# A shared feed-forward stage by pairs of token tiles: inner rows made transposed, logits in four column groups

## What is computed

```python
logits = xf @ w_gate.T                                  # 4096 x 8
scores = softmax(logits)
...                                                     # top groups, top 2 experts
shared = silu(xf @ sw1.T) * (xf @ sw3.T) @ sw2.T        # 512 -> 512 -> 512
out = shared.at[flat_idx].add(routed_out)
x = x + out
```

## Time and profile before

| | |
|---|---|
| median of 3 runs | 2368.78 us (2368.17 to 2370.43) |
| profiled execution, its own time | 2368.74 us |
| its span | 2367.0 us |
| TensorE matmul busy | 2099.7 us, 89% of the span |
| VectorE, ScalarE, GpSimd busy | 1451.2, 1072.9, 671.0 us |
| mean granted TensorE clock | 0.957 of full speed |
| the shared stage, first turn of x to last row out | 1922.7 to about 2253 us |

### The profile page before, as it was taken

The page is one execution under the profiler, slowest core; times in us unless marked ns, Lnnn a source line. Parts: engine busy times, 40 slices in busy tenths (PEclk is TensorE's granted clock), DMA queues, the critical chain, the costliest instruction groups (busy, mean ns, idle before and its releaser), DMA issues. The chain is left out here.

```text
span 2367.0 us, 47476 instructions
## 1 busy us (share of the span) xinstructions
PE 2099.7 (89%) x14941; PEld 1593.7 (67%) x14976; DVE 1451.2 (61%) x4087; ACT 1072.9 (45%) x2781; POOL 671.0 (28%) x1179
## 2 busy tenths in 40 slices
PE   5998999899998379898995899999999979999986
PEld 4777777677776344444443788888888768888844
DVE  5777777777777377777773565655655533333354
ACT  4566566556656533333342445444454422222224
POOL 1233233223322355555552221212212111111100
PEclk8999999999999589999997899999999989999999
DMA  5011121111100611212114012112121083222100
GB/s 173 31 47 39 47 66 38 38 68 45 38 23 23 231 50 54 66 53 66 58 53 152 29 37 73 64 44 72 36 72 54 28 280 118 74 79 76 66 10 0
DMA packets 91344, 158.11 MB, mean 67 GB/s; under 512 B 11248, under 2 KB 21488, under 8 KB 90752
## 3 DMA queue, kind: packets, MB, share of 16 engines
q1 hardware_dynamic: 91264, 157.10, 19.5%
HBM read 123.50 MB, written 33.57 MB: 66 GB/s over the span
## 5 line engine op out<-in xcount | busy, mean ns | idle before, releaser
L480 ACT ACTIVATE a_probs<-a_probs,a_negm 128x256 f32<-128x256 f32 x512 | 254.3, 504 | 179.1 <-DVE a_negm L581 179.1
L400 POOL TENSOR_SCALAR a_probs<-a_probs,a_rinv 128x256 f32<-128x256 f32 x256 | 130.3, 524 | 467.2 <-DVE a_rinv L597 467.0
L581 DVE CUSTOM_DVE_ANT_0 a_probs<-a_s,a_mbias 128x256 f32<-128x256 f32 x512 | 188.6, 417 | 12.7 <-PE a_s L801 12.7
L818 PE MATMUL a_pt<-a_ident,a_probs 128*128 128x128 f32 x1024 | 160.8, 281 | 19.3 <-DVE a_pT L590 7.8
L1125 ACT ACTIVATE b_raw<-b_g,b_xs 128x512 f32<-128x512 f32 x128 | 88.1, 688 | 181.9 <-PE b_g L1296 181.9
L1296 PE MATMUL b_u<-b_wu,b_raw 128*128 128x512 bf16 x495 | 130.7, 380 | 40.1 <-DVE b_raw L1208 39.2
L480 ACT ACTIVATE c_probs<-c_probs,c_negm 128x256 f32<-128x256 f32 x256 | 127.4, 502 | 83.2 <-DVE c_negm L581 83.2
L400 POOL TENSOR_SCALAR c_probs<-c_probs,c_rinv 128x256 f32<-128x256 f32 x128 | 64.9, 522 | 326.6 <-DVE c_rinv L597 326.4
L818 PEld LDWEIGHTS a_pt<-a_ident,a_probs 128*128 128x128 f32 x1024 | 124.1, 144 | 45.6 <-issue 22.9
L767 PE MATMUL a_x<-a_wo,a_oT 128*128 128x512 f32 x384 | 114.4, 447 | 23.8 <-DVE a_xnT L627 23.8
L1208 DVE SCALAR_TENSOR_TENSOR b_raw<-b_u,b_xs,b_raw 128x512 f32<-128x512 f32 x128 | 93.0, 745 | 62.2 <-ACT b_raw L1125 54.7
(11 more groups left out here) (297 smaller groups left out, 4981.1 us busy)
## 6 DMA issues: line engine op xcount, KB each, us to landing
m_ew<-in_L_ffn_w_dram SPq DMA_DIRECT2D x24, 512.0 KB, 8.9
a_cbuf<-in_ctx_dram SPq DMA_DIRECT2D x16, 512.0 KB, 5.3
a_xbuf<-in_x_dram SPq DMA_DIRECT2D x16, 512.0 KB, 4.2
a_resb<-in_x_dram SPq DMA_DIRECT2D x16, 512.0 KB, 3.6
x<-a_resb SPq DMA_DIRECT2D x16, 512.0 KB, 2.8
b_xbuf<-x SPq DMA_DIRECT2D x32, 256.0 KB, 2.7
b_raw<-x SPq DMA_DIRECT2D x32, 256.0 KB, 2.8
x<-b_raw SPq DMA_DIRECT2D x32, 256.0 KB, 2.0
```

Source lines behind the costliest of these rows:

```text
L400: last = nc.gpsimd.tensor_scalar(pr, pr, rinv[:, s, QT + t:QT + t + 1], 0.0, ALU.mult, ALU.add)
L480: nc.scalar.activation(pr, pr, ACT.Exp, bias=negm[:, s, h % 2, t:t + 1], scale=-1.0, accum_out=ssum[:, s, QT * (h % 2) + t:QT * (h % 2) + ...
L581: nc.vector.tensor_tensor_reduce(out=probs[:, s, h % 2, t], in0=s_bank[h][:, t * SEQ:(t + 1) * SEQ], in1=mbias[:, el.par], scale=-sm_scale ...
L818: last = nc.tensor.transpose(pt_bank[:, kt * SEQ + t * P:kt * SEQ + (t + 1) * P], probs[:, s, m, t, kt * P:(kt + 1) * P], ident[:])
```

## The change

The stage now works on 16 groups of two tiles (256 tokens).

- `gate` and `up` are made transposed: the weights are stationary (128 inner features at a time) and the 256 token columns of a pair move. Each is cut into two halves of 256 features (`features`), 24 matmuls of 256 columns a half. What `hidden` makes is thus already what `down` needs as stationary operand; `turn_h` and the bank `th` are gone, and `hi_h` and `lo_h` read `hid` from memory.
- `xnT` holds both tiles of a pair side by side, and `gate` of a pair's first half waits for `tx_lo` of both tiles.
- The logits are made transposed: `gateT` is padded to 32 columns and stationary, and the four chunks of 128 features go to the four groups of 32 columns of the array, into 128 partitions of the bank `lT`. ScalarE copies it (`logits_out`), and `fold_logits` adds up the four parts with a matmul by `fold`, which GpSimd now makes in this stage.
- Each tile of a pair has its own bank for `down`, `z0` and `z1`. x is loaded six tiles ahead, not four.

The diff, cut to its core, with the code's left margin taken off:

```diff
-gateT = tsb("gateT", [P, KC, EXPERTS])
+gateT = tsb("gateT", [P, KC, 32])
...
-xnT = tsb("xnT", [P, 2, 2, DIM], F32R)
-xnT_full = tsb("xnT_full", [P, 2, DIM])
+GROUP = 2 * P
+xnT = tsb("xnT", [P, 2, 2, KC, GROUP], F32R)
+xnT_full = tsb("xnT_full", [P, KC, GROUP])
+logitsT = tsb("logitsT", [P, GROUP])
...
-hidT = tsb("hidT", [P, 2, 2, DIM], F32R)
-tx_bank, th_bank, g_bank, u_bank, z_bank = [tbank(n) for n in ("tx", "th", "g", "u", "z")]
-w_bank = [tx_bank, th_bank, g_bank, u_bank]
+hidT = tsb("hidT", [P, 2, KC, GROUP], F32R)
+tx_bank, lT_bank, g_bank, u_bank = [tbank(n) for n in ("tx", "lT", "g", "u")]
+z_bank = [tbank("z0"), tbank("z1")]
+w_bank = [tx_bank, z_bank[1], g_bank, u_bank]
...
         def iteration(el):
-            if el.has(4):
-                load_x(el.plus(4))
+            if el.has(6):
+                load_x(el.plus(6))
...
-        def hi_h(el):
-            act.wait_ge(th_done, el.n + 1)
-            nc.scalar.activation(hidT[:, el.par, HI], th_bank[:], ACT.Copy).then_inc(th_hi, 1)
...
+        def hi_x(el, t):
+            n, cut = 2 * el.n + t, slice(t * P, (t + 1) * P)
+            act.wait_ge(tx_done, n + 1)
+            wait_for(act, lT_done, el.n)
+            src = tx_bank[:].rearrange("p (k n) -> p k n", k=KC)
+            nc.scalar.activation(xnT_full[:, :, cut], src, ACT.Copy).then_inc(tx_full, 1)
+            nc.scalar.activation(xnT[:, el.par, HI, :, cut], src, ACT.Copy).then_inc(tx_hi, 1)
...
+        def hi_h(el, half):
+            act.wait_ge(h_done, el.n * 2 + half + 1)
+            nc.scalar.activation(hidT[:, HI, 2 * half:2 * half + 2].rearrange("p j n -> p (j n)"),
+                                 hid[:, half], ACT.Copy).then_inc(h_hi, 1)
+
+        def logits_out(el):
+            act.wait_ge(lT_done, el.n + 1)
+            wait_for(act, lg_done, el.n)
+            nc.scalar.activation(logitsT[:], lT_bank[:, 0:GROUP], ACT.Copy).then_inc(lT_out, 1)
...
         def iteration(el):
-            if el.has(1):
-                silu(el.plus(1))
-            hi_h(el)
+            if not el.has(1):
+                return
+            silu(el.plus(1), 0)
+            logits_out(el.plus(1))
+            hi_h(el.plus(1), 0)
             if el.has(2):
-                hi_x(el.plus(2))
-
-        run_elements(act, tiles, iteration, ahead=4)
+                hi_x(el.plus(2), 0)
+            silu(el.plus(1), 1)
+            hi_h(el.plus(1), 1)
+            if el.has(2):
+                hi_x(el.plus(2), 1)
+
+        run_elements(act, groups, iteration)
...
+        def lo_x(el, t):
+            n, cut = 2 * el.n + t, slice(t * P, (t + 1) * P)
+            dve.wait_ge(tx_hi, n + 1)
+            nc.vector.tensor_tensor(xnT[:, el.par, LO, :, cut], tx_bank[:].rearrange("p (k n) -> p k n", k=KC),
+                                    xnT[:, el.par, HI, :, cut].bitcast(F32), ALU.subtract).then_inc(tx_lo, 1)
+
+        def hidden(el, half):
+            n = el.n * 2 + half
+            dve.wait_ge(silu_done, n + 1)
+            dve.wait_ge(u_done, n + 1)
+            wait_for(dve, h_hi, n - 1)
+            nc.vector.tensor_tensor(hid[:, half], u_bank[:], act_gate[:, half], ALU.mult).then_inc(h_done, 1)
+
+        def lo_h(el, half):
+            dve.wait_ge(h_hi, el.n * 2 + half + 1)
+            hi, lo = (hidT[:, part, 2 * half:2 * half + 2].rearrange("p j n -> p (j n)") for part in (HI, LO))
+            nc.vector.tensor_tensor(lo, hid[:, half], hi.bitcast(F32), ALU.subtract).then_inc(h_lo, 1)
+
+        def rows_out(el, t):
+            dve.wait_ge(r_loaded[t], el.n * 16 + 16)
+            dve.wait_ge(z_done, el.n * 2 + t + 1)
+            nc.vector.tensor_tensor(resb[:, t], z_bank[t][:], resb[:, t], ALU.add).then_inc(out_done, 1)
...
         def iteration(el):
-            lo_h(el)
-            if el.has(1):
-                hidden(el.plus(1))
-            if el.has(2):
-                lo_x(el.plus(2))
-            if el.has(3):
-                row_stats(el.plus(3))
-            rows_out(el)
+            rows_out(el, 0)
             if isinstance(el.n, int) and el.n == 0:
                 keep_first()
-
-        run_elements(dve, tiles, iteration, ahead=4)
+            rows_out(el, 1)
+            if not el.has(1):
+                return
+            hidden(el.plus(1), 0)
+            lo_h(el.plus(1), 0)
+            if el.has(2):
+                lo_x(el.plus(2), 0)
+            if el.has(3):
+                row_stats(Element(el.plus(3).n, 0, tiles))
+            hidden(el.plus(1), 1)
+            lo_h(el.plus(1), 1)
+            if el.has(2):
+                lo_x(el.plus(2), 1)
+            if el.has(3):
+                row_stats(Element(el.plus(3).n, 1, tiles))
+
+        run_elements(dve, groups, iteration, ahead=4)
...
+        def features(el, half, bank, w, done, read):
+            wait_for(pe, read, el.n * 2 + half)
+            for m in range(2):
+                j = 2 * half + m
+                for k in range(KC):
+                    for a, b in TERMS:
+                        last = nc.tensor.matmul(bank[:, m * GROUP:(m + 1) * GROUP],
+                                                w[:, b, k, j * P:(j + 1) * P], xnT[:, el.par, a, k],
+                                                start=(k == 0 and (a, b) == TERMS[0]),
+                                                stop=(k == KC - 1 and (a, b) == TERMS[-1]))
             last.then_inc(done, 1)
 
-        def turn_x(el):
-            pe.wait_ge(xn_ready, el.n + 1)
-            wait_for(pe, tx_lo, el.n)
-            turn(tx_bank, xn[:, el.par], tx_done)
-
-        def turn_h(el):
-            pe.wait_ge(h_done, el.n + 1)
-            wait_for(pe, th_lo, el.n)
-            turn(th_bank, hid[:, el.par], th_done)
-
-        def product(bank, srcT, w, done):
+        def gate(el, half):
+            if half == 0:
+                pe.wait_ge(tx_lo, 2 * el.n + 2)
+            features(el, half, g_bank, sw[0], g_done, silu_done)
+
+        def up(el, half):
+            features(el, half, u_bank, sw[1], u_done, h_done)
+
+        def logits(el):
+            pe.wait_ge(tx_full, 2 * el.n + 2)
+            wait_for(pe, lT_out, el.n)
+            for k in range(KC):
+                last = nc.tensor.matmul(lT_bank[32 * k:32 * k + 32, 0:GROUP], gateT[:, k], xnT_full[:, k],
+                                        start=True, stop=True, skip_group_check=True)
+            last.then_inc(lT_done, 1)
+
+        def fold_logits(el):
+            pe.wait_ge(lT_out, el.n + 1)
+            pe.wait_ge(fold_ready, 3)
+            for t in range(2):
+                n = 2 * el.n + t
+                last = nc.tensor.matmul(lg_bank[:, bass.ds(n * EXPERTS, EXPERTS)],
+                                        logitsT[:, t * P:(t + 1) * P], fold[:], start=True, stop=True)
+            last.then_inc(lg_done, 1)
+
+        def down(el, t):
+            pe.wait_ge(h_lo, el.n * 2 + 2)
+            wait_for(pe, out_done, el.n * 2 + t - 1)
             for k in range(KC):
                 for a, b in TERMS:
-                    last = nc.tensor.matmul(bank[:], srcT[:, a, k * P:(k + 1) * P], w[:, b, k],
+                    last = nc.tensor.matmul(z_bank[t][:], hidT[:, a, k, t * P:(t + 1) * P], sw[2][:, b, k],
...
+            last.then_inc(z_done, 1)
+
+        for t in range(2):
+            turn_x(first_group[0], t)
+        gate(first_group[0], 0)
+        logits(first_group[0])
+        up(first_group[0], 0)
+        fold_logits(first_group[0])
+        turn_x(first_group[1], 0)
+        gate(first_group[0], 1)
+        up(first_group[0], 1)
+        turn_x(first_group[1], 1)
 
         def iteration(el):
             if el.has(1):
+                gate(el.plus(1), 0)
                 logits(el.plus(1))
-                gate(el.plus(1))
-            turn_h(el)
+            down(el, 0)
             if el.has(1):
-                up(el.plus(1))
+                fold_logits(el.plus(1))
+            down(el, 1)
+            if el.has(1):
+                up(el.plus(1), 0)
             if el.has(2):
-                turn_x(el.plus(2))
-            down(el)
-
-        run_elements(pe, tiles, iteration, ahead=4)
+                turn_x(el.plus(2), 0)
+            if el.has(1):
```

More of the change, by code:

```diff
@@ L1379, in routed_ffn_phase @@
         first_ready = sem("first_ready")
+        fold = sb("fold", [P, EXPERTS])
+        fold_ready = sem("fold_ready")
         with ExitStack() as shared:
@@ L1420, in routed_ffn_phase @@
                          "r_loaded1 stored0 stored1 bn_done stats_ready ln_step xn_ready tx_done tx_hi tx_full "
-                         "tx_lo lg_done g_done u_done silu_done h_done th_done th_hi th_lo z_done out_done").split()]
+                         "tx_lo lT_done lT_out lg_done g_done u_done silu_done h_done h_hi h_lo z_done out_done").split()]
                 x_loaded, r_loaded, stored = (x_loaded0, x_loaded1), (r_loaded0, r_loaded1), (stored0, stored1)
                 w_loaded = [sem(f"sw_loaded{n}") for n in range(3)]
```

(30 more changed lines are left out.)

103 lines of the change are left out of this document (44 added, 59 removed).

## The result

The changed kernel takes 2438.74 us (median of 5 runs, 2436.81 to 2440.99) against 2370.14 of the kernel before on the same chip: ratio 1.0293, 95% interval 1.0278 to 1.0308, slower by 69 us. The forecast was slower by 48. Its mechanism is there, but the time lies 7 us above its range (2397 to 2432): the change costs some 20 us more than forecast, most of it at one place.

A forecast was written before the change was run, and what follows sets the result against it. TensorE's own stream was taken to bound the stage, 20.1 us a pair. Work -18, stall +45, clock falls +19 and edges +2 gave +48 us on 2368.74: 2417 us, range 2397 to 2432.

The forecast's parts named there:

- TensorE's work: Changed loop, matmul stream of a pair without waits: 19.0 us against 20.1, a gain of 18 us for 16 pairs.
- The stall: `gate` opening an iteration waits for the split of the x just turned: 3.0 us a pair, 15 times, 45 us.
- the chain named: From the second tile's turn: `hidden`, `hi_h`, second copy of x, `lo_x`, then `gate` 3.36 us after the turn starts.
- a stall of 2.1: Least wait before `gate`, if `hi_h` were not ahead: the chain from the turn alone, 0.64 + 1.81 us.
- The price of a fall: After a stall TensorE's clock may drop to half level; 3.4 us of that costs 1.6 us.
- The number: Clock falls expected behind the stalls before `gate`: 12 in 15, 19 us in all, bounds 0 and 47.
- Edges: Start and end of the stage: first `gate` 2.6 us later, 1.4 regained, 0.7 more before the last `down`; +2 us.
- Edges and the rest: Prediction's section on stage start and end, other engines and loads: +2 us for the edges, nothing for SyncE's x loads.
- The clock stays whole: Rival: the stalls before `gate` cause no clock falls, all else as forecast; 2398 us, chance 15%.
- The stall is hidden: Rival: the x split ends within the turn, so `gate` does not wait and the kernel gets faster; 2353 us, chance 3%.
- The weight loads show: Rival: the `gate` and `up` halves' extra weight loads are not hidden; 77 us more, 2494 us, chance 2%.
- It does not do what it says: Rival: time unchanged, only by a chance tie of gain and loss at a stall of 1.2 us; chance 2%.

The follow-up runs named there:

- run 4: Kernel of run 2 with ScalarE's copies of the second tile ahead of its copy of the second hidden half, and VectorE's `lo_x` ahead of `lo_h`: 2403.72 us.
- run 3: Kernel of run 2 plus 13 useless matmuls of 512 columns behind the last turn of each iteration, into a bank nobody reads: 2407.10 us.
- run 1: Changed kernel with SyncE's loads of x for tiles 4 and 5 issued ahead of the eight `w2` loads: 2425.03 us.
- run 2: Changed kernel with VectorE's prologue statistics of tile 4 after `hidden`, `lo_h` and `lo_x` of the first pair: 2425.64 us.
- run 9: Changed kernel with the edits of run 1 and run 2, and the residual rows of tile 1 loaded ahead of `w2` too: 2419.44 us.
- run 5: Kernel of run 2 with the second turn of x ahead of the second `up` half, and its copies and `lo_x` ahead of the second hidden half's split: 2371.37 us.
- run 7: Kernel of run 5 with the x loads of tiles 4 and 5 ahead of the `w2` loads, as in run 1: 2363.01 us.

## Why the prediction was right, and where not

- **TensorE's work: 19.0 us a pair, measured 19.10** (22.10 by starts, less the stall's 3.00). The parts are: halves 3.08 with the switch back from the wait, 2.84, 2.92 and 2.85, two `down` 2.88 and 2.87, logits 0.57 (forecast 0.75), fold 0.37 (0.40), turns 0.36 each. The logits were cheaper, the first half is 0.27 longer than the 2.81 of the earlier trace rows and the other three 0.03 to 0.11, and each `down` 0.04 to 0.05 longer than 2.83. Against the forecast 1.6 us in all.
- **The stall: 3.0, measured 3.00** (3.36 from turn to `gate` less 0.36). Right, and run 4 shows that the chain named is the one that counts: with `hi_h` behind, turn to `gate` is 2.50 (1942.89 to 1945.39), less 0.36 a stall of 2.14, where the prediction had "a stall of 2.1".
- **The price of a fall: 1.6, measured 1.6** (23.72 against 22.10). **The number: 12, it was 14.** 3 us. That the clock falls at all, could not decide; run 3 shows that the falls cost time, 15 to 18 us there.
- **Edges: +2.** `gate` began 5.87 us after the first turn and not 2.82, 3.0 later (2.6 forecast), and the matmuls that met the low clock gave 0.9 back; before the last `down` 2.23 us idle and not 1.41, 0.8 more (0.7). That is 2.9 in all.
- **The step that failed** is a wait put at nothing, in "Edges and the rest": "SyncE issues the same DMAs with x loaded six tiles ahead, not four; x has two buffers still, so a load waits as before ... Nothing." When the load is *issued* did not change (1948.45 and 1949.07), as that step said. It said nothing of when it *lands*, behind eight `w2` loads, 10.5 us later, nor of what is queued behind the statistics on VectorE: `hidden`, and so `gate`. The loop was costed from a pair in its middle, and the prologue, where VectorE's order is written out separately, was looked at for TensorE's waits alone. It cost 18.42 - 2.76 = **15.7 us**. Runs 1, 2 and 9 show it.

The sum: 48 forecast, 15.7 for this wait, 3.2 for two falls, 1.6 for the work is 68.5, and 69.4 with the edges as measured; the stage is 68.0 longer, the median 68.6. The terms are rounded, so an agreement to some 1.5 us is all that this shows.

**The rivals.** *The clock stays whole* is refuted: idle pieces of 2.76 us were followed by the half level 13 times in 14. The rule of the Trainium skill that the prediction weighed ("TensorE: Matmul & The Clock Gate", "Why this matters for your kernels": no idle gap above some 3 us) would leave the clock whole at such a length; it is not borne out in this stream, and run 4 goes further, with 8 in 15 at 1.90. *The stall is hidden* did not happen in the change; the fifth run makes it true, and would have given 2353 by the forecast's 1.1 us a pair. It gave 2371, and 2360 with the loads put right. Part of the rest is the pair: 19.43 us and not 19.0, of which 0.3 comes with the turn between two halves. *The weight loads show* is refuted by halves of 2.84 to 2.92. *It does not do what it says* needed a stall of 1.2 us, and it was 3.00.

Open: why two halves beside a turn take 0.3 us more (in the rows of run 7, 0.12 us lie between the end of `gate` and the turn, the rest is in longer matmul groups), which of the stalls the clock answers with a fall, and what moves the stage's start by up to 6 us.

## What to carry to other kernels

When an iteration's last product is the next one's first operand, cost the whole chain from the turn to the use, with everything queued ahead of it on the copying engines, and then look for a block of TensorE work to put in between: here that was worth 54 us (run 5 against run 2). Cost the prologue apart from the loop: for each wait that an engine takes there, ask where the DMA stands in its queue, when it lands, and what stands behind the waiting instruction. A wait that was harmless can become the longest of the kernel when one critical instruction is moved behind it.

## What the hardware showed that was not expected

- TensorE with 182 matmuls more was 18.5 us faster; its granted clock was 1.00 for the 313.8 us of the window.
- After idle pieces of equal length the clock sometimes fell and sometimes not: 2.76 us in the change 13 of 14, in run 1 12 of 14, in run 2 11 of 15, in run 9 13 of 15, and 1.90 us 8 of 15. In the earlier trace rows no single piece of such a length stood in steady work; these do, with about 19.3 us of it between them.
- Four FP32 matmuls in four column groups (eight records) took 0.57 us to the next start. The forecast had 0.17 for a switch by the earlier trace rows; where no wait stands ahead (run 7), the `gate` before them took 2.94, against 2.88 for the `up` halves of steady pairs, which leaves less than 0.1.
- 256 KB of x issued behind eight loads of `w2` landed after 10.5 us in both kernels; in steady work the same load landed after 2.7 us and cost VectorE no wait at all.
